# A router that exponentiates all six logits on GpSimd, and output rounding, residual adds and normalization at other steps of the feed-forward loop

## The chip, the cores and the metric

One core of a Trainium2 chip runs the whole program. The metric is the device time of one execution in microseconds (us); lower is better. The engines are named as in the profile: PE (TensorE matmul), PEld (its weight load), DVE (VectorE), ACT (ScalarE), POOL (GpSimd), SP (SyncE, which only issues DMA here).

## What is computed

Two transformer layers over x of 4 x 1024 tokens with 256 features: cross-attention, a mixture of six experts, a second cross-attention, and a quantized feed-forward part, each on a layer-normalized x and each added to x. What matters here are the router and the last part:

```
z = x @ proj_w.T ; q = tanh(z / 0.3) ; dot = q @ anchors.T
logits = -(6 - dot) * 0.5 / clip(routing_temp, 0.1)
topk_logits, topk_idx = top_k(logits, 2)
topk_w = softmax(topk_logits)            # weight 0 for the other four experts
out = sum over e of  gelu(x @ w1[e]) @ w2[e] * weight[e]
...
h = round256(x @ w1 + b1) ; h = round256(piecewise_linear_gelu(h))
out = round256(h @ w2 + b2) ; x = x + out
```

## The kernel before

The 4096 tokens are eight blocks g = 0 to 7 of 512 tokens (NT = 4 tiles of 128 partitions). x stays in SBUF. Four stages follow one another: attention (to about 245 us of the span), experts (250 to 430), attention again (430 to 617), feed-forward (617 to the end). Each engine's program is written out by hand, in order; engines wait for each other on semaphores only, and each engine issues strictly in its written order.

**Experts.** Per block, for e = 0 to 5: PE computes `hidden` (6 matmuls, line 141) and, two experts behind, `output` (12 matmuls, line 640); ACT applies Gelu twice; DVE or POOL forms the low part (`rest` line 598, `rest_pooled` line 509); DVE's `add` (line 608, four instructions a call) adds the expert's output, scaled by the routing weight, into x. PE's `output` of expert e waits until `add` of expert e-1 has emptied the bank. The router of a block is DVE's `router` (in the step e = 0, lines 562 to 578): logits, ten comparisons that give each logit's `rank`, the maximum `top`, `below` = logit - top, and, by way of `second` (rank equal 1, times below) and a sum, `gap`, one number per token: how far the second logit lies below the first. POOL's `power` (line 515) raises e to `gap`, 128x4 elements. DVE's `share` (step e = 2, behind `rest` of that step and ahead of `add` of expert 0, lines 584 to 591) makes the six weights of it: ex at rank 1, 1 at rank 0, over 1 + ex. POOL's other `pow` is line 103, the inverse square root of the normalization, also 128x4, with the product `shift` (line 105) behind it.

**Feed-forward.** The loop runs over k = 0 to 63, with g, c = divmod(k, 8): block g, hidden slice c of 128. "Step c" below is one turn of that loop on one engine. A slice goes: PE `hidden(k)` (6 matmuls, L141), DVE `early(k)` (fixed, L753), ACT two Gelus (fg, L728, L729), POOL `climb(k)` (frise, L711), DVE `interpolate(k)` (fpart, L759), POOL `grow(k)` (fy, L718; on DVE, L765, for c = 1 and 4), ACT `leading(k)` (L735, L738), DVE `rest(k)` (fyl, L771), PE `output(k)` (12 matmuls, L804). In step k the engines do: DVE early(k), interpolate(k-2), rest(k-4), then finish(k-2) where that is DVE's; ACT gelus(k), leading(k-3); POOL climb(k), grow(k-1); PE hidden(k), output(k-6). PE's hidden(k) waits for early(k-2), since two banks are in turn.

Between these stand the pieces of other blocks. DVE's `moments` for block g+2 (stats, L90) is in step 2, POOL's `invert` (L103, L105) in step 4, ACT's `norm` for block g+2 (xn, L114, four tiles) in steps 6 and 7, two tiles each. PE turns the normalized block (`norm.turn`, four transposes, L127) in step 1 of the next block and again in step 5; ACT takes them over with `lead` (L132) first thing in steps 2 and 6, DVE with `norm.rest` (L136) first thing in steps 3 and 7. PE's first hidden of a block needs both. When the outputs of a block are all summed, ACT's `round_output` (fr, L744, two instructions) and then DVE's `ff.add` (x, L780, two instructions) finish it: for block g-2 in step 2 and step 4 of block g. SP stores the block after the add.

Of the kernel before, what the change touches and what calls it, by code (L numbers as in the profile page):

```python
# [16 lines left out]
P = 128  # L17
# [415 lines left out]
class Experts:  # L433
# [5 lines left out]
    def __init__(self, nc, sem, place, norm, ps, m):  # L439
# [23 lines left out]
        self.euler = small("euler", [P, NT, 1], F32)  # L463
# [3 lines left out]
        self.gap, self.ex = small("gap", [P, NT, 1], F32), small("ex", [P, NT, 1], F32)  # L467
        self.exs, self.second = small("exs", [P, NT, E], F32), small("second", [P, NT, E], F32)
# [44 lines left out]
    def power(self, pool, g):  # L513
        pool.wait_ge(self.below_ready, g + 1)
        self.nc.gpsimd.tensor_tensor(self.ex[:], self.euler[:], self.gap[:], ALU.pow).then_inc(self.ex_ready, 1)
        pool.wait_ge(self.ex_ready, g + 1)
# [42 lines left out]
    def router(self, dve, g):  # L559
        nc = self.nc  # L560
        dve.wait_ge(self.dot_done, g + 1)
        nc.vector.tensor_scalar(self.logit[:], self.RD[:, 0:NT * E].rearrange("p (t e) -> p t e", e=E), 6.0, self.half[:, 0:1],
                                ALU.subtract, ALU.mult).then_inc(self.logit_ready, 1)
        dve.wait_ge(self.logit_ready, g + 1)
        for o in range(E):
            for lo, hi, op in ((0, o, ALU.is_gt), (o + 1, E, ALU.is_ge)):
                if lo < hi:
                    self.put(nc.vector.tensor_tensor(self.above[:, :, lo:hi, o], self.logit[:, :, o:o + 1].to_broadcast([P, NT, hi - lo]),
                                                     self.logit[:, :, lo:hi], op))
        self.put(nc.vector.reduce_max(self.top[:], self.logit[:], AX.X))  # L570
        dve.wait_ge(self.router_chain, self.chain)
        self.put(nc.vector.reduce_sum(self.rank[:], self.above[:], AX.X))
        self.put(nc.vector.tensor_tensor(self.below[:], self.logit[:], self.top[:].to_broadcast([P, NT, E]), ALU.subtract))
        dve.wait_ge(self.router_chain, self.chain)
        self.put(nc.vector.scalar_tensor_tensor(self.second[:], self.rank[:], 1.0, self.below[:], ALU.is_equal, ALU.mult))
        dve.wait_ge(self.router_chain, self.chain)
        need(dve, self.ex_ready, g)
        nc.vector.reduce_sum(self.gap[:], self.second[:], AX.X).then_inc(self.below_ready, 1)

    def share(self, dve, g):  # L580
# [3 lines left out]
        self.put(nc.vector.scalar_tensor_tensor(self.second[:], self.rank[:], 1.0, self.ex[:].to_broadcast([P, NT, E]), ALU.is_equal,  # L584
                                                ALU.mult))
        self.put(nc.vector.tensor_scalar(self.total[:], self.ex[:], 1.0, None, ALU.add))
        dve.wait_ge(self.router_chain, self.chain)
        self.put(nc.vector.scalar_tensor_tensor(self.exs[:], self.rank[:], 0.0, self.second[:], ALU.is_equal, ALU.add))
# [245 lines left out]
def build(nc, d, out):  # L834
    m, at0, at1 = memory_map()
    place = Places(nc)
    with ExitStack() as stack:
# [48 lines left out]
        with nc.Block() as block:  # L886
# [219 lines left out]
            def _(act):  # L1106
# [138 lines left out]
                for k in range(BLOCKS * FC):  # L1245
# [9 lines left out]
                    if k < 2:  # L1255
                        norm.norm(act, LN_FFN + 1, range(2 * k, 2 * k + 2))
                    elif c >= FC - 2 and g + 2 < BLOCKS:
                        norm.norm(act, LN_FFN + g + 2, range(2 * (c - FC + 2), 2 * (c - FC + 3)))
                    if c == 2 and g > 1:
                        ff.round_output(act, g - 2)  # L1260
                    if k == BLOCKS * FC - 1:
                        ff.round_output(act, g - 1)
# [5 lines left out]
            def _(dve):  # L1268
# [160 lines left out]
                for k in range(BLOCKS * FC):  # L1429
# [16 lines left out]
                    if c == 4 and g > 1:  # L1446
                        ff.add(dve, g - 2)
# [262 lines left out]
```

## Time and profile before

| | us |
|---|---|
| median of 3 runs (840.4 to 841.5) | 840.44 |
| the profiled execution | 840.4 |
| its span, first to last instruction | 838.6 |
| busy: PE / DVE / ACT / POOL | 756.9 / 673.2 / 521.0 / 352.4 |
| mean granted TensorE clock | 0.979 |

The profile is of one execution. Its span leaves 1.8 us of its time outside the first and last instruction. In a timeline row the columns are start, duration, engine, line, operation, what is written from what, and in brackets how long the engine sat idle before it and what released it. A pipelined matmul's duration overlaps the next one's, so the distance between starts is what counts.

### The profile page before, as it was taken

What the parts mean: (1) busy time and instruction counts of PE and PEld (TensorE: products, weight loads), DVE (VectorE), ACT (ScalarE), POOL (GpSimd) and SP (SyncE); (2) the same over time, 40 slices, a digit from 0 to 9 for tenths busy, and PEclk for the clock granted to TensorE, in tenths of its full rate; (3) what the DMA queues carried; (4) which work ended last, traced back from release to release, by engine and by line L of the source; (5) the groups of instructions that cost most, each with busy time, mean ns of one, the idle gap of its engine ahead of it and who ended that gap; (6) DMA issues with size and microseconds to landing.
All of it is one profiled execution on the core that took longest, in us unless ns stands there. A gap on an engine that the chain in (4) does not pass through costs nothing.

```text
span 838.6 us, 13625 instructions
## 1 busy us (share of the span) xinstructions
PE 756.9 (90%) x4388; PEld 555.8 (66%) x4388; DVE 673.2 (80%) x1614; ACT 521.0 (62%) x943; POOL 352.4 (42%) x309
## 2 busy tenths in 40 slices
PE   3799999999989999999979898888888989988995
PEld 2566566665558888888854555444457978887885
DVE  7657777777877878888886888887869898889896
ACT  4355555555654446554445766666659878988875
POOL 5433322233112222233231222232238988988984
PEclk9899999999999999999987999999999999999999
DMA  7975633564110000001084555754200000000001
GB/s 221 153 181 115 140 65 65 109 113 92 54 33 1 1 1 6 2 1 52 1 125 67 65 76 78 127 73 56 29 1 2 1 26 1 26 27 26 26 11 65
DMA packets 24957, 48.51 MB, mean 58 GB/s; under 512 B 3670, under 2 KB 6871, under 8 KB 24376
## 3 DMA queue, kind: packets, MB, share of 16 engines
q1 hardware_dynamic: 23366, 46.54, 28.9%
q10 hardware_dynamic: 1522, 1.11, 0.4%
q8 instruction: 36, 0.59, 0.3%
q14 instruction: 33, 0.27, 0.1%
HBM read 11.99 MB, written 4.19 MB: 19 GB/s over the span
## 4 chain that ended last, share of the span: by engine, by line
PE 53%; DVE 20%; issue 9%; ACT 7%; DMA 5%; POOL 4%; DVEq 0%; ACTq 0%; POOLq 0%
PE bank L141 15%; PE bank L640 6%; PE bank L377 6%; PE bank L427 6%; PE bank L402 6%; DMA qst<-mt 5%; PE bank L413 4%; DVE mx L333 4%; PE bank L804 3%; PE bank L405 2%; DVE x L608 2%; PE bank L127 2%; DVE fpart L759 2%; POOL fy L718 2%; PE bank L380 2%
## 5 line engine op out<-in xcount | busy, mean ns | idle before, releaser
L307 ACT ACTIVATE pt<-bank 77x512 f32<-77x512 f32 x256 | 146.5, 589 | 119.6 <-PE bank L405 73.2
L333 DVE TENSOR_REDUCE mx<-bank 128x4 f32<-128x308 f32 x256 | 109.2, 471 | 30.6 <-PE bank L380 17.8
L402 PE MATMUL bank<-qst,l_kst 128*77 128x512 f32 (+1 forms) x256 | 107.3, 432 | 19.8 <-DMA qst<-mt 14.0
L377 PE MATMUL bank<-l_kblk,qh 128*128 128x308 f32 x256 | 90.7, 372 | 12.6 <-DVE mx L333 9.0
L711 POOL TENSOR_TENSOR frise<-fg,fg 128x512 f32<-128x512 f32 x64 | 96.1, 1502 | 7.5 <-ACT fg L729 2.7
L402 PEld LDWEIGHTS bank<-qst,l_kst 128*77 128x77 f32 (+1 forms) x256 | 36.9, 149 | 84.0 <-issue 47.6
L377 PEld LDWEIGHTS bank<-l_kblk,qh 128*128 128x128 f32 x256 | 50.7, 199 | 55.9 <-issue 45.7
L103 POOL TENSOR_TENSOR rstd<-var,minus_half 128x4 f32<-128x4 f32 x32 | 34.4, 1075 | 120.5 <-DVE var L98 67.5
L608 DVE SCALAR_TENSOR_TENSOR x<-bank,eweight,x 128x256 f32<-128x256 f32 x192 | 79.5, 476 | 4.6 <-PE bank L640 4.3
L718 POOL TENSOR_TENSOR fy<-fpart,fg 128x512 f32<-128x512 f32 x48 | 72.6, 1513 | 19.4 <-DVE fpart L759 8.7
L283 POOL TENSOR_TENSOR ol<-ot,oh 128x512 fp32r<-128x512 f32 x32 | 41.5, 1296 | 92.6 <-ACT oh L312 60.4
L804 PE MATMUL bank<-fw2h,fyh 128*128 128x256 f32 x256 | 72.5, 283 | 3.4 <-DVE fyl L771 3.3
L413 PE MATMUL bank<-pt,l_vall 128*32 128x512 f32 x512 | 69.3, 613 | 4.7 <-DVE ut L341 2.0
L114 ACT ACTIVATE xn<-x,shift,rstd 128x256 f32<-128x256 f32 (+1 forms) x128 | 66.9, 589 | 10.8 <-POOL shift L105 10.8
L804 PE MATMUL bank<-fw2l,fyh 128*128 128x256 f32 x256 | 72.1, 282 | 0.0
L804 PE MATMUL bank<-fw2h,fyl 128*128 128x256 f32 x256 | 71.9, 281 | 0.0
L759 DVE SCALAR_TENSOR_TENSOR fpart<-ffixed,frise 128x512 f32<-128x512 uint16 x64 | 55.3, 864 | 15.1 <-POOL frise L711 15.0
L141 PE MATMUL bank<-fxh,fw1h 128*128 128x512 f32 x128 | 52.6, 411 | 12.2 <-DVE fxl L136 7.2
L640 PE MATMUL bank<-ew2h,ehh 128*128 128x256 f32 x192 | 56.5, 294 | 2.8 <-DVE x L608 2.8
L728 ACT ACTIVATE fg<-ffixed 128x512 f32<-128x512 int16 x64 | 40.2, 628 | 23.8 <-DVE ffixed L753 23.6
L509 POOL TENSOR_TENSOR ehl<-eh,ehh 128x512 fp32r<-128x512 f32 x16 | 20.7, 1294 | 81.2 <-ACT ehh L525 81.2
L640 PE MATMUL bank<-ew2l,ehh 128*128 128x256 f32 x192 | 54.7, 285 | 0.0
(181 smaller groups left out, 2125.2 us busy)
## 6 DMA issues: line engine op xcount, KB each, us to landing
qst<-qh SPq DMA_DIRECT2D x64, 256.0 KB, 6.8
qst<-ql SPq DMA_DIRECT2D x32, 256.0 KB, 9.0
out<-x SPq DMA_DIRECT2D x8, 512.0 KB, 2.6
qst<-ml SPq DMA_DIRECT2D x8, 480.0 KB
x<-in_x SPq DMA_DIRECT2D x3, 1024.0 KB, 12.5
weights<-in_mlp_w SPq DMA_DIRECT2D x2, 1024.0 KB, 5.0
mraw<-in_mask SPq DMA_DIRECT2D x8, 154.0 KB
x<-in_x SPq DMA_DIRECT2D x2, 512.0 KB, 5.9
```

Of the source, the lines that this page charges most:

```text
L141: last = self.nc.tensor.matmul(out, w, a, start=(first and k == 0), stop=(k == len(ops) - 1))
L307: self.nc.scalar.activation(self.pt[0:T, i // 4 % 2, i % 4, :], self.bank_of(G, i)[0:T, :], ACT.Exp).then_inc(self.probs, 1)
L333: self.nc.vector.reduce_max(out, banks[u % len(banks)][:, 0:4 * T].rearrange("q (p par t) -> q p par t", p=2, par=2), AX.X).then_inc(self. ...
L377: last = self.nc.tensor.matmul(bank, self.qh[:, c, tile], keys, start=True, stop=not layer.masked)
L402: last = self.nc.tensor.matmul(out, layer.kst[rows, layer.stack(c * HC + 2 * k + par), b * T:(b + 1) * T], self.qst[rows, self.slot(G), c ...
L413: last = self.nc.tensor.matmul(self.U[32 * k:32 * k + 32, :], layer.vall[:, self.batch(G), layer.value(c * HC + 2 * k + par), :], self.pt[ ...
L608: last = self.nc.vector.scalar_tensor_tensor(tile, part, self.weight[:, g % 2, 2 * k + t, e:e + 1], tile, ALU.mult, ALU.add)
L640: last = self.nc.tensor.matmul(self.OUT[k][:, t * D:(t + 1) * D], a[:, e % self.R, tile], w[:, e, :], start=(j == 0), stop=(j == 2))
L711: self.nc.gpsimd.tensor_tensor(self.rise[:, k % 2, :], self.g1[:, k % self.R, :], self.g0[:, k % self.R, :], ALU.subtract).then_inc(self.r ...
L718: self.nc.gpsimd.tensor_tensor(self.y[:, k % 2, :], self.part[:, k % 2, :], self.g0[:, k % self.R, :], ALU.add).then_inc(self.y_ready[0], 1)
L759: self.nc.vector.scalar_tensor_tensor(self.part[:, k % 2, :], self.fractions[:, k % self.R, :, 0], 2.0 ** -16, self.rise[:, k % 2, :], ALU ...
L804: last = nc.tensor.matmul(self.OUT[2 * (g % 2) + t // 2][:, t % 2 * D:(t % 2 + 1) * D], a[:, k % self.R, t * P:(t + 1) * P], w[:, c, :], s ...
```

## The change

Router: `gap` and `second` are gone. POOL's pow takes `below` itself, so 128x24 elements (all six logits of each token) and not 128x4, with `euler` as wide. `share` keeps the values where rank is under 2, sums the six, inverts the sum and multiplies.

Feed-forward: ACT normalizes one tile in step 6, one in step 7, and the last two in step 0 of the next block (before: two and two in steps 6 and 7). ACT's `round_output` of block g-1 stands in step 7 of block g, behind that tile (before: step 2 of block g+1). DVE's `ff.add` of block g-2 stands in step 0 of block g (before: step 4).

```diff
-        self.euler = small("euler", [P, NT, 1], F32)
+        self.euler = small("euler", [P, NT, E], F32)
...
-        self.gap, self.ex = small("gap", [P, NT, 1], F32), small("ex", [P, NT, 1], F32)
-        self.exs, self.second = small("exs", [P, NT, E], F32), small("second", [P, NT, E], F32)
+        self.ex, self.exs = small("ex", [P, NT, E], F32), small("exs", [P, NT, E], F32)
...
-        self.nc.gpsimd.tensor_tensor(self.ex[:], self.euler[:], self.gap[:], ALU.pow).then_inc(self.ex_ready, 1)
+        self.nc.gpsimd.tensor_tensor(self.ex[:], self.euler[:], self.below[:], ALU.pow).then_inc(self.ex_ready, 1)
...
         self.put(nc.vector.reduce_sum(self.rank[:], self.above[:], AX.X))
-        self.put(nc.vector.tensor_tensor(self.below[:], self.logit[:], self.top[:].to_broadcast([P, NT, E]), ALU.subtract))
-        dve.wait_ge(self.router_chain, self.chain)
-        self.put(nc.vector.scalar_tensor_tensor(self.second[:], self.rank[:], 1.0, self.below[:], ALU.is_equal, ALU.mult))
-        dve.wait_ge(self.router_chain, self.chain)
         need(dve, self.ex_ready, g)
-        nc.vector.reduce_sum(self.gap[:], self.second[:], AX.X).then_inc(self.below_ready, 1)
+        nc.vector.tensor_tensor(self.below[:], self.logit[:], self.top[:].to_broadcast([P, NT, E]),
+                                ALU.subtract).then_inc(self.below_ready, 1)
...
-        self.put(nc.vector.scalar_tensor_tensor(self.second[:], self.rank[:], 1.0, self.ex[:].to_broadcast([P, NT, E]), ALU.is_equal,
-                                                ALU.mult))
-        self.put(nc.vector.tensor_scalar(self.total[:], self.ex[:], 1.0, None, ALU.add))
+        self.put(nc.vector.scalar_tensor_tensor(self.exs[:], self.rank[:], 2.0, self.ex[:], ALU.is_lt, ALU.mult))
         dve.wait_ge(self.router_chain, self.chain)
-        self.put(nc.vector.scalar_tensor_tensor(self.exs[:], self.rank[:], 0.0, self.second[:], ALU.is_equal, ALU.add))
+        self.put(nc.vector.reduce_sum(self.total[:], self.exs[:], AX.X))
+        dve.wait_ge(self.router_chain, self.chain)
         self.put(nc.vector.reciprocal(self.rtotal[:], self.total[:]))
...
                     if k < 2:
                         norm.norm(act, LN_FFN + 1, range(2 * k, 2 * k + 2))
+                    elif c == 0 and g + 1 < BLOCKS:
+                        norm.norm(act, LN_FFN + g + 1, range(2, NT))
                     elif c >= FC - 2 and g + 2 < BLOCKS:
-                        norm.norm(act, LN_FFN + g + 2, range(2 * (c - FC + 2), 2 * (c - FC + 3)))
-                    if c == 2 and g > 1:
-                        ff.round_output(act, g - 2)
-                    if k == BLOCKS * FC - 1:
+                        norm.norm(act, LN_FFN + g + 2, range(c - FC + 2, c - FC + 3))
+                    if c == FC - 1 and g > 0:
                         ff.round_output(act, g - 1)
...
-                    if c == 4 and g > 1:
+                    if c == 0 and g > 1:
                         ff.add(dve, g - 2)
```

On DVE, the router and the share of block 0 before, from `below` on (line 358 is a residual add of the attention, only in block 0):

```order
L573 TENSOR_TENSOR ebelow<-elogit,etop 128x24
L575 SCALAR_TENSOR_TENSOR esecond<-erank,ebelow 128x24
L578 TENSOR_REDUCE egap<-esecond 128x4
L598 TENSOR_TENSOR ehl<-eh,ehh 128x512
L358 TENSOR_TENSOR x<-x,bank 128x512 x2
L598 TENSOR_TENSOR ehl<-eh,ehh 128x512
L584 SCALAR_TENSOR_TENSOR esecond<-erank,eex 128x24
L586 TENSOR_SCALAR etotal<-eex 128x4
L588 SCALAR_TENSOR_TENSOR eexs<-erank,esecond 128x24
L589 RECIPROCAL ertotal<-etotal 128x4
L591 TENSOR_TENSOR eweight<-eexs,ertotal 128x24
```

and the same place of the change:

```order
L573 TENSOR_TENSOR ebelow<-elogit,etop 128x24
L593 TENSOR_TENSOR ehl<-eh,ehh 128x512
L358 TENSOR_TENSOR x<-x,bank 128x512 x2
L593 TENSOR_TENSOR ehl<-eh,ehh 128x512
L580 SCALAR_TENSOR_TENSOR eexs<-erank,eex 128x24
L582 TENSOR_REDUCE etotal<-eexs 128x4
L584 RECIPROCAL ertotal<-etotal 128x4
L586 TENSOR_TENSOR eweight<-eexs,ertotal 128x24
```

Two instructions ahead of the pow and one in the share are gone; three of the share's four now each need the one before.

On ACT, from the end of step 6 to the end of step 7 before:

```order
L114 ACTIVATE xn<-x,shift,rstd 128x255 x2
L728 ACTIVATE fg_154<-ffixed 128x512
L729 ACTIVATE fg_155<-ffixed,fsegment 128x512
L735 ACTIVATE bank<-fy 128x512
L738 ACTIVATE fyh<-bank 128x512
L114 ACTIVATE xn<-x,shift,rstd 128x255 x2
```

and of the change, from the end of step 6 to the end of step 0:

```order
L114 ACTIVATE xn<-x,shift,rstd 128x255
L723 ACTIVATE fg_152<-ffixed 128x512
L724 ACTIVATE fg_153<-ffixed,fsegment 128x512
L730 ACTIVATE bank<-fy 128x512
L733 ACTIVATE fyh<-bank 128x512
L114 ACTIVATE xn<-x,shift,rstd 128x255
L739 ACTIVATE fr<-bank 128x512 x2
L723 ACTIVATE fg_152<-ffixed 128x512
L724 ACTIVATE fg_153<-ffixed,fsegment 128x512
L730 ACTIVATE bank<-fy 128x512
L733 ACTIVATE fyh<-bank 128x512
L114 ACTIVATE xn<-x,shift,rstd 128x255 x2
```

Two of the four tiles have moved behind leading of step 0, and the two roundings (fr) stand in step 7, where before they stood three steps later.

On DVE, steps 3 (its end) and 4 of a block before:

```order
L765 TENSOR_TENSOR fy<-fpart,fg_154 128x512
L753 TENSOR_SCALAR ffixed<-bank 128x512
L759 SCALAR_TENSOR_TENSOR fpart<-ffixed,frise 128x512
L771 SCALAR_TENSOR_TENSOR fyl<-bank,fyh 128x512
L780 SCALAR_TENSOR_TENSOR x<-fr,x 128x512 x2
```

and steps 0, 1 and the beginning of 2 of the change:

```order
L748 TENSOR_SCALAR ffixed<-bank 128x512
L754 SCALAR_TENSOR_TENSOR fpart<-ffixed,frise 128x512
L766 SCALAR_TENSOR_TENSOR fyl<-bank,fyh 128x512
L775 SCALAR_TENSOR_TENSOR x<-fr,x 128x512 x2
L748 TENSOR_SCALAR ffixed<-bank 128x512
L754 SCALAR_TENSOR_TENSOR fpart<-ffixed,frise 128x512
L766 SCALAR_TENSOR_TENSOR fyl<-bank,fyh 128x512
```

The two adds into x now stand between rest of step 0 and early of step 1.

## Rows read from the trace of the kernel before

**Rows 1.** Busy time by stage: stretch, its length, each engine's busy time, clock, DMA.

```profile
250.00:420.00 170.00, 167.21 (x1053) 142.04 (x1054) 141.51 (x490) 86.59 (x164) 45.90 (x46) 1.00 0.03 9
640.00:800.00 160.00, 148.56 (x947) 133.33 (x947) 141.15 (x239) 136.24 (x244) 140.48 (x98) 1.00 0.05 18
```

**Rows 2.** Waits of PE, 250 to 420 us: total, times, longest.

```profile
PE bank L640 <- DVE x L608: 2.8, 8, 1.2
```

**Rows 3.** Timeline of DVE, share of block 2, router and share of block 3.

```profile
300.58 0.17 DVE L584 SCALAR_TENSOR_TENSOR esecond<-erank,eex 128x24 f32<-128x24 f32 x1
...
317.99 0.17 DVE L573 TENSOR_TENSOR ebelow<-elogit,etop 128x24 f32<-128x24 f32 x1
318.20 0.18 DVE L575 SCALAR_TENSOR_TENSOR esecond<-erank,ebelow 128x24 f32<-128x24 f32 x1
...
318.51 0.68 DVE L598 TENSOR_TENSOR ehl<-eh,ehh 128x512 fp32r<-128x512 f32 x1
...
321.73 0.18 DVE L584 SCALAR_TENSOR_TENSOR esecond<-erank,eex 128x24 f32<-128x24 f32 x1
321.82 0.16 DVE L586 TENSOR_SCALAR etotal<-eex 128x4 f32<-128x4 f32 x1
322.02 0.19 DVE L588 SCALAR_TENSOR_TENSOR eexs<-erank,esecond 128x24 f32<-128x24 f32 x1
...
322.54 1.66 DVE L608 SCALAR_TENSOR_TENSOR x<-bank,eweight,x 128x256 f32<-128x256 f32 x4
```

**Rows 4.** Timeline of POOL, 265 to 320 us.

```profile
269.17 1.01 POOL L103 TENSOR_TENSOR rstd<-var,minus_half 128x4 f32<-128x4 f32 x1 [2.35 <-issue]
270.25 0.32 POOL L105 TENSOR_TENSOR shift<-minus_mean,rstd 128x4 f32<-128x4 f32 x1
...
295.42 1.32 POOL L515 TENSOR_TENSOR eex<-eeuler,egap 128x4 f32<-128x4 f32 x1 [2.60 <-DVE egap L578]
...
318.74 1.32 POOL L515 TENSOR_TENSOR eex<-eeuler,egap 128x4 f32<-128x4 f32 x1 [2.76 <-DVE egap L578]
```

**Rows 5.** Timeline of DVE, feed-forward, blocks 1 to 3, and the tail.

```profile
649.78 1.40 DVE L90 BATCH_NORM_STATS2 stats<-x 128x6 f32<-128x256 f32 x4
...
670.39 0.69 DVE L759 SCALAR_TENSOR_TENSOR fpart<-ffixed,frise 128x512 f32<-128x512 uint16 x1 [1.20 <-POOL frise L711]
...
673.66 0.69 DVE L759 SCALAR_TENSOR_TENSOR fpart<-ffixed,frise 128x512 f32<-128x512 uint16 x1 [1.24 <-POOL frise L711]
...
674.87 1.39 DVE L90 BATCH_NORM_STATS2 stats<-x 128x6 f32<-128x256 f32 x4
...
682.73 3.16 DVE L780 SCALAR_TENSOR_TENSOR x<-fr,x 128x512 f32<-128x512 f32 x2
685.80 0.68 DVE L753 TENSOR_SCALAR ffixed<-bank 128x512 int32<-128x512 f32 x1
...
701.41 1.39 DVE L90 BATCH_NORM_STATS2 stats<-x 128x6 f32<-128x256 f32 x4
...
829.74 1.28 DVE L780 SCALAR_TENSOR_TENSOR x<-fr,x 128x512 f32<-128x512 f32 x2
```

**Rows 6.** Timeline of PE, same stretch: a turn of step 1, and its two stalls.

```profile
669.59 0.60 PE L127 MATMUL bank<-ident,xn 128*128 128x128 f32 x4
...
686.63 0.47 PE L141 MATMUL bank<-fxh,fw1h 128*128 128x512 f32 x1 [1.49 <-DVE ffixed L753]
...
690.99 0.50 PE L141 MATMUL bank<-fxh,fw1h 128*128 128x512 f32 x1 [1.30 <-DVE fxl L136]
```

**Rows 7.** Timeline of ACT: end of step 7, start of steps 0 and 1, block 2.

```profile
667.76 1.08 ACT L114 ACTIVATE xn<-x,shift,rstd 128x255 f32<-128x255 f32 x2
668.75 0.62 ACT L728 ACTIVATE fg<-ffixed 128x512 f32<-128x512 int16 x1
...
670.99 0.62 ACT L728 ACTIVATE fg<-ffixed 128x512 f32<-128x512 int16 x1
```

**Rows 8.** Timeline of POOL: the climbs of steps 2 and 3, block 2.

```profile
678.33 3.32 POOL L711 TENSOR_TENSOR frise<-fg,fg 128x512 f32<-128x512 f32 x2
```

## The prediction

> **What bounds the kernel now.** I read the stretches first. In the expert stage PE is busy 167.2 of 170 us and POOL only 45.9 [rows 1]; PE's only wait there is for DVE's add of expert 0, 2.8 us in eight waits [rows 2]. So anything that delays that add adds to the time one for one, and what shortens DVE's or POOL's own work gives almost nothing. In the feed-forward all four engines are busy 85 to 93% [rows 1], so none bounds it alone and the timelines must be read step by step. Block 1 has no ff.add; from its statistics to those of block 2 are 674.87 - 649.78 = 25.09 us. From there on every block has an add, and 701.41 - 674.87 = 26.54 us pass [rows 5]. The add of step 4, 3.16 us on DVE [rows 5], therefore costs 1.45 us a block. It holds up early of step 5 (685.80), and with it PE's hidden of step 7 (stall 1.49) and, by way of the late norm.rest, the first hidden of the next block (1.30) [rows 6].
>
> **Router, ahead of the pow.** The issue distances are 0.21 us for an instruction that waits for the one before and 0.10 for one that doesn't. Two instructions go: from below to the next ehl are 318.51 - 317.99 = 0.52 us [rows 3], afterwards 0.10. The pow is released 0.42 us sooner in each of 8 blocks. DVE's own 3.4 us are worth nothing, since PE doesn't wait for DVE there.
>
> **Share.** Before: five instructions, 322.54 - 321.73 = 0.81 us, two of them side by side (0.09 and 0.10, the others 0.20 and more) [rows 3]. After: four, each waiting for the one before, 4 x 0.21 = 0.84. Neutral; it stands ahead of the add that PE waits for, so 8 x 0.03 = 0.2 us lost at most.
>
> **The pow, six times as wide.** This is the open price. Trace: 1.32 us for 128x4 in the router, 1.01 for 128x4 in the normalization; the product of 128x4 right behind takes 0.32 [rows 4]. No wider pow is in the trace. Lower end: all of it is fixed, and 20 more columns cost what a subtraction's columns cost on POOL (3.32 us for two of 512 columns [rows 8], 3 ns each): 1.38 us. Upper end: all but the 0.32 of an instruction as such grows with the columns: (1.32 - 0.32) x 6 + 0.32 = 6.3; if the 0.31 by which the router's pow exceeds the other is a wait for a shared access and stays fixed, (1.01 - 0.32) x 6 + 0.63 = 4.8. What covers it: in block 3 the pow starts at 318.74, the share at 321.73: 2.99 us, and 0.42 more from the earlier release, so a pow up to 3.4 us is free. In block 2 it is 300.58 - 295.42 + 0.42 = 5.6 [rows 3, 4]. I count seven blocks like block 3 and one like block 2. The cost is 7 x (d - 3.4): nothing up to 3.4 us, 9.8 us at 4.8, 7 x 2.9 + 0.7 = 21.0 at 6.3. Of these ends neither is nearer to a row: each is the 128x4 row carried on by another assumption. I take the middle between 1.38 and 4.8, 3.1 us, which is just covered, so a cost of nothing; that stands for about 0.4 us of set-up in the pow beside the 0.32, the rest growing with the columns. It is a choice and not a finding, and both ends stay in the range.
>
> The Trainium skill ("GPSIMD Engine Reference", section 2.1) says that a GpSimd tensor_tensor is an ordinary loop over the elements in software. The trace agrees for subtraction (3 ns a column over 512) and has no second width for pow. By that rule pow's extra would lie in the loop: the first rival below, whose price is worked out from the rows above.
>
> **ff.add to step 0.** What it gives where it leaves: at most the 1.45 us a block above, six blocks (2 to 7), 8.7 us. What it costs where it goes: in steps 1 and 2 of a block DVE waits 1.20 and 1.24 us for POOL [rows 5]. The add (3.16) uses these 2.44 and pushes step 2's moments back 0.5 to 0.7. POOL isn't hurt at once: grow of step 0 starts well over 2 us after the interpolation it needs. The adds could run in 1.28 us together, as in the tail where POOL has stopped [rows 5], but steps 7 to 2 are where POOL is never idle, so I keep 3.16. The add also waits for the roundings, now one step ahead of it on ACT and not two: 0.2 us.
>
> **Norm and rounding on ACT.** Steps 6 and 7 lose two tiles (1.0 us), step 7 gets the two roundings (1.0), so Gelu of step 0 starts about where it did, 668.8 to 669.3 [rows 7]. Before, normalization was complete at 668.8 and PE turned at 669.59 without a wait [rows 6]. Now the last two tiles stand behind the plain step of 670.99 - 668.75 = 2.24 us [rows 7] and take 1.0: complete at about 672.6. PE stands still some 3 us in its step 1, a new wait, and behind it is hidden of step 2, done at 674.6. DVE's early of step 2 would have come at 673.5 (its delay by the add counted), so it slips another 1.1; moments then are 1.6 late, early of step 3 too, and POOL, whose climb of step 3 follows that of step 2 directly [rows 8], waits 1.2 for it. Then step 4 has no add: early of step 5 comes at 684.5, not 685.80 (gain 1.3). Working the same steps through the next block with the same durations I get 710.2 against 685.80 + 26.54 = 712.34 (0.8 more). PE profits later, because the stall of 3 us has taken the place of the 1.49 and 1.30: its first hidden of block 3 comes at 690.7 against 690.99, that of block 4 at 717.1 against 717.53 (0.4). For blocks 4, 5 and 6 I take DVE's 0.8 each: 2.9 us when block 7 starts. Block 7 has no norm and no turn, its add is mostly covered before and after: 0.5. Sum 3.4 us. Store DMAs go out four steps sooner, and nothing waits for them but the end, whose last add doesn't move. The tail is the same.
>
> **Sum.** Profiled execution 840.4 (median 840.44, the same), of it span 838.6: minus 3.4 for the feed-forward, plus 0 for the pow, plus 0.2 for the share: **837.2 us**.
>
> **Rivals.** (1) *The pow is a loop.* Against it: only a guess on set-up. For it: nearly 0.7 us more than a product for only four columns. From d = 3.4 on, share waits for POOL, add of expert 0 waits behind it, and PE's output of expert 1 stands. At d = 4.0 the cost is 4.2 and the whole 841.4; at 4.8 it is 9.8 and 847.0; at 6.3 it is 21.0 and 858.2. Slower than before from d = 3.9 on. (2) *The add is wholly absorbed*, the turn's wait falling in PE's slack: 25.09 a block, 8.7 gained, 831.9. For it: in block 1 to 2 PE ran a whole block with no stall. Against: ACT's order puts two tiles on the turn's path in every block. (3) *The turn is the new bound.* PE needs 26.54 - 1.49 - 1.30 = 23.75 a block without stalls; with all 3 us of the turn's wait kept, 26.75, 0.2 more than before: 841.6 in all. It decides if ACT's steps 7 and 0 run no earlier relative to PE than now.
>
> **How the numbers follow.** Forecast with a cheap pow (836 to 839): 0.43. Rival 1: 0.33, of it a third below 841 (the feed-forward's gain pays), a third 841 to 846, a third above. Rival 2: 0.12. Rival 3: 0.12, near 840 to 842. About 0.2%, 1.7 us, is what a measurement can tell from no change. Faster than 838.7: 0.40 of the forecast, 0.12, and 0.03 of rival 1, that is 0.55. Within 0.2% (838.7 to 842.1): 0.03 + 0.10 + 0.08 = 0.21. Slower: 0.20 + 0.04 = 0.24. The range 833 to 847 leaves out a part of rival 2 (0.07) and the upper end of rival 1 (0.10).
>
> **What would show it.** The pow's duration in the changed trace, against 3.4; a wait of share's first instruction for POOL, or PE's wait for L608's successor above 0.35 each. In the feed-forward: a wait of DVE's first moved add for ACT's rounding (0.2 us), PE waiting 2 to 3 us at the transposes of step 1, the two stalls of rows 6 gone, and statistics to statistics 25.7 us. The prediction is wrong if the pow takes over 4 us, or if the turn's wait is either absent or adds to the old stalls.

## The result and the profile after

The changed kernel takes 850.15 us (median of five runs, 847.73 to 856.15) against 841.5 us of the kernel before (five runs, 840.4 to 843.17): a ratio of 1.0101, interval 1.0065 to 1.0137. It is slower by about 8.6 us, outside the predicted range. Its profiled execution took 849.2 us, of it a span of 847.4. The time given with a run is the median of all its executions; its ratio, and every count of clocks below, leaves out those more than 1.5% above the fastest of the same kernel, six in all: two of some 1403 us, and four of kernels with the new feed-forward order, at mean clocks of 0.966 to 0.970, so that the ratios rather flatter that order.

From the first router logits to the last, the expert stage took 401.13 - 249.98 = 151.15 us before and 410.77 - 253.03 = 157.74 now: 6.6 us more. Four of the seven blocks between them take 1.36 to 1.39 us more, two 0.29 and 0.77, one nothing; the share of the last block, behind the last logits, waits too and adds 1.4, which makes 8.0 us. From the first statistics of the feed-forward to the last add: 834.27 - 626.31 = 207.96 us before, 843.06 - 637.26 = 205.80 now, 2.2 us less. The stage ahead of both, whose code is the same, ended 3.05 us later in this trace; the traces of this study with that stage unchanged put the moment anywhere from 249.98 to 253.8, so this is variation between executions and no effect. The three make up the difference of the two profiled executions: 3.05 + 8.0 - 2.2 = 8.85 us, against 849.2 - 840.4 = 8.8.

Against [rows 1], the same two stretches of the changed kernel (stretch, its length, busy time of PE, PEld, DVE, ACT, POOL with the number of instructions, granted clock, DMA):

```profile
250.00:420.00 170.00, 159.68 (x1001) 134.52 (x1000) 131.77 (x441) 84.97 (x161) 70.98 (x44) 1.00 0.02 8
640.00:800.00 160.00, 146.81 (x936) 131.89 (x937) 150.16 (x243) 140.19 (x249) 137.86 (x99) 1.00 0.05 18
```

In the expert stage PE is busy 7.5 us less and POOL 25 us more. Against [rows 2], the waits of PE and then of DVE in the expert stage (total, times, longest):

```profile
PE bank L635 <- DVE x L603: 10.3, 9, 1.5
```

```profile
DVE ehl L593 <- ACT ehh L524: 23.0, 22, 2.7
DVE eexs L580 <- POOL eex L514: 7.0, 7, 1.2
```

PE's wait for the add of expert 0 went from 2.8 us to 10.3, and DVE has a new wait, for the pow, in seven of eight blocks. Against [rows 3, 4], the line of the pow, its duration in ns (shortest, median, longest):

```profile
L514 POOL TENSOR_TENSOR eex<-eeuler,ebelow x8: 4167/4700/4704, 254.9 to 412.6; 128x24 f32<-128x24 f32 x8
```

And one block, POOL, DVE and PE, each row with start and duration, and in brackets the idle time ahead of it and what ended it:

```profile
323.05 4.70 POOL L514 TENSOR_TENSOR eex<-eeuler,ebelow 128x24 f32<-128x24 f32 x1 [2.34 <-DVE ebelow L573]
```

```profile
322.73 0.17 DVE L573 TENSOR_TENSOR ebelow<-elogit,etop 128x24 f32<-128x24 f32 x1
323.04 0.69 DVE L593 TENSOR_TENSOR ehl<-eh,ehh 128x512 fp32r<-128x512 f32 x1
...
327.78 0.18 DVE L580 SCALAR_TENSOR_TENSOR eexs<-erank,eex 128x24 f32<-128x24 f32 x1 [1.24 <-POOL eex L514]
328.00 0.18 DVE L582 TENSOR_REDUCE etotal<-eexs 128x4 f32<-128x24 f32 x1
328.21 0.18 DVE L584 RECIPROCAL ertotal<-etotal 128x4 f32<-128x4 f32 x1
328.43 0.18 DVE L586 TENSOR_TENSOR eweight<-eexs,ertotal 128x24 f32<-128x24 f32 x1
328.64 0.48 DVE L603 SCALAR_TENSOR_TENSOR x<-bank,eweight,x 128x256 f32<-128x256 f32 x1
```

```profile
329.67 0.36 PE L635 MATMUL bank<-ew2h,ehh 128*128 128x256 f32 x1 [1.50 <-DVE x L603]
```

The chain is the one of the first rival: pow, DVE's wait of 1.24 us, four chained share instructions 0.22, 0.21, 0.22 and 0.21 us apart, the add, and 1.50 us of PE standing still.

In the feed-forward, PE's turns against [rows 6] (step 1 of block 1, step 5, and step 1 of block 2), its waits, and DVE and POOL at the places of [rows 5, 8]:

```profile
658.05 0.65 PE L127 MATMUL bank<-ident,xn 128*128 128x128 f32 x4 [1.16 <-ACT xn L114]
669.77 0.60 PE L127 MATMUL bank<-ident,xn 128*128 128x128 f32 x4
683.87 0.66 PE L127 MATMUL bank<-ident,xn 128*128 128x128 f32 x4 [1.79 <-ACT xn L114]
```

```profile
PE bank L127 <- ACT xn L114: 10.3, 6, 1.9
PE bank L799 <- DVE fyl L766: 3.8, 5, 1.3
```

```profile
687.91 1.40 DVE L90 BATCH_NORM_STATS2 stats<-x 128x6 f32<-128x256 f32 x4
...
706.03 2.39 DVE L775 SCALAR_TENSOR_TENSOR x<-fr,x 128x512 f32<-128x512 f32 x2 [0.28 <-ACT fr L739]
...
711.85 0.69 DVE L748 TENSOR_SCALAR ffixed<-bank 128x512 int32<-128x512 f32 x1 [1.14 <-PE bank L141]
...
713.69 1.39 DVE L90 BATCH_NORM_STATS2 stats<-x 128x6 f32<-128x256 f32 x4
```

```profile
718.39 1.57 POOL L706 TENSOR_TENSOR frise<-fg,fg 128x512 f32<-128x512 f32 x1 [1.33 <-ACT fg L724]
```

The two old stalls of 1.49 and 1.30 us [rows 6] are gone, PE waits up to 1.9 us at the turn of step 1 instead, and a block takes 713.69 - 687.91 = 25.78 us where it took 26.54 [rows 5].

### The profile page after: what moved, and what is told of

Its sections match the earlier page's. It is cut to its first block, busy times and chain, and to the rows that moved or that the text cites. A ratio compares the mean times of both kernels' runs of the same rounds, so it can differ in the third digit from the quotient of the medians.

```text
span 847.4 us, 13594 instructions
## 1 busy us (share of the span) xinstructions
PE 758.7 (90%) x4388; PEld 556.8 (66%) x4388; DVE 671.9 (79%) x1590; ACT 521.9 (62%) x943; POOL 377.9 (45%) x309
## 4 chain that ended last, share of the span: by engine, by line
PE 54%; DVE 19%; POOL 8%; issue 7%; ACT 6%; DMA 6%; ACTq 0%; DVEq 0%; POOLq 0%
PE bank L141 15%; PE bank L402 6%; PE bank L377 5%; PE bank L427 5%; PE bank L635 5%; DMA qst<-mt 5%; PE bank L413 4%; DVE mx L333 4%; POOL eex L514 4%; PE bank L799 4%; PE bank L405 2%; DVE fpart L754 2%; PE bank L127 2%; POOL frise L706 2%; DVE x L603 2%
## 5 line engine op out<-in xcount | busy, mean ns | idle before, releaser
L706 POOL TENSOR_TENSOR frise<-fg,fg 128x512 f32<-128x512 f32 x64 | 99.2, 1550 | 13.4 <-ACT fg L724 8.9
L713 POOL TENSOR_TENSOR fy<-fpart,fg 128x512 f32<-128x512 f32 x48 | 67.6, 1408 | 13.5 <-DVE fpart L754 10.2
L754 DVE SCALAR_TENSOR_TENSOR fpart<-ffixed,frise 128x512 f32<-128x512 uint16 x64 | 61.8, 966 | 9.2 <-POOL frise L706 9.2
L635 PE MATMUL bank<-ew2h,ehh 128*128 128x256 f32 x192 | 56.6, 295 | 10.3 <-DVE x L603 10.3
L635 PE MATMUL bank<-ew2h,ehl 128*128 128x256 f32 x192 | 54.5, 284 | 0.0
L522 ACT ACTIVATE eh<-bank 128x512 f32<-128x512 f32 x48 | 28.7, 597 | 39.7 <-PE bank L141 38.6
L799 PEld LDWEIGHTS bank<-fw2h,fyh 128*128 128x128 f32 x256 | 48.3, 189 | 7.2 <-DVE fyl L766 4.8
```

The source lines that it names most:

```text
L635: last = self.nc.tensor.matmul(self.OUT[k][:, t * D:(t + 1) * D], a[:, e % self.R, tile], w[:, e, :], start=(j == 0), stop=(j == 2))
L706: self.nc.gpsimd.tensor_tensor(self.rise[:, k % 2, :], self.g1[:, k % self.R, :], self.g0[:, k % self.R, :], ALU.subtract).then_inc(self.r ...
L713: self.nc.gpsimd.tensor_tensor(self.y[:, k % 2, :], self.part[:, k % 2, :], self.g0[:, k % self.R, :], ALU.add).then_inc(self.y_ready[0], 1)
L754: self.nc.vector.scalar_tensor_tensor(self.part[:, k % 2, :], self.fractions[:, k % self.R, :, 0], 2.0 ** -16, self.rise[:, k % 2, :], ALU ...
L799: last = nc.tensor.matmul(self.OUT[2 * (g % 2) + t // 2][:, t % 2 * D:(t % 2 + 1) * D], a[:, k % self.R, t * P:(t + 1) * P], w[:, c, :], s ...
```

## The experiments

A period below is the distance from one block's statistics to the next one's; "feed-forward" is the distance from its first statistics to the last add; ratios, with their 95% interval, are to the kernel before on the same chip, so that two runs on different chips compare by their ratios and not by their times.

### Which half costs

**The router half alone**: the exponentials of the changed kernel, the feed-forward of the kernel before.

```
-        self.nc.gpsimd.tensor_tensor(self.ex[:], self.euler[:], self.gap[:], ALU.pow)
+        self.nc.gpsimd.tensor_tensor(self.ex[:], self.euler[:], self.below[:], ALU.pow)
```

> The kernel before with the router's half of the change alone: pow on 128x24, share of four instructions, feed-forward untouched. Theory 'pow duration': the pow takes 4.7 us where 3.34 are covered, so about 1.37 us in each of seven blocks less a looser block 2, near +8 us over the kernel before (ratio 1.009 to 1.010); PE's waits for DVE's scaled add in the expert stage sum to about 10 us and not 2.8. Rival 'two halves in conflict': the loss comes from the feed-forward half or from both together, and this kernel is less than 4 us slower.

850.93 us, ratio 1.0101 (1.0081 to 1.0121). First to last logits 157.71 us, feed-forward 207.91 as before; PE's wait for the add 10.3 us. The whole loss of the change is here.

**The feed-forward half alone**, with the router of before.

```
+                    elif c == 0 and g + 1 < BLOCKS:
+                        norm.norm(act, LN_FFN + g + 1, range(2, NT))
...
-                        norm.norm(act, LN_FFN + g + 2, range(2 * (c - FC + 2), 2 * (c - FC + 3)))
-                    if c == 2 and g > 1:
-                        ff.round_output(act, g - 2)
-                    if k == BLOCKS * FC - 1:
+                        norm.norm(act, LN_FFN + g + 2, range(c - FC + 2, c - FC + 3))
+                    if c == FC - 1 and g > 0:
+                        ff.round_output(act, g - 1)
...
-                    if c == 4 and g > 1:
+                    if c == 0 and g > 1:
```

> The kernel before with the feed-forward half alone: tiles 1, 1, 2 in steps 6, 7, 0, rounding in step 7, add in step 0. Theory: the changed kernel's trace has the stretch from the first feed-forward statistics to the last add 2.2 us shorter (205.8 against 208.0), so this kernel is 2 us faster than the one before (ratio 0.997 to 0.998). Rival: the gain of the trace is a product of the later start and the kernel is within 1 us of before; or the half costs and explains part of the loss.

842.2 us, ratio 0.9988 (0.9967 to 1.001): no difference that this can tell. Its profiled execution took 838.49 us, with 151.15 us of experts and a feed-forward of 205.72, so 2.2 us shorter, as expected. The whole series gained less than that one execution and than the 0.997 to 0.998 expected, and the later copies of this kernel, below, show one reason.

**Adds and roundings moved, normalization where it was**, and **the normalization moved alone**.

> The kernel before with rounding in step 7 and the add in step 0, but all four tiles normalized in steps 6 and 7 as before. Theory: the turn of PE's step 1 no longer waits 1.8 us for ACT in each block and block 1 loses nothing, so this is faster than the feed-forward half whole: 3 to 6 us under the kernel before, statistics to statistics near 25.3 us. Rival: two tiles and two roundings in step 7 (about 4.3 us of ACT) are too much for one step; the Gelu of step 0 and the wait of the add for the rounding come a us later, and it is no faster than the feed-forward half whole.

> The kernel before with the tiles moved alone (1, 1, 2 in steps 6, 7, 0), rounding in step 2 and add in step 4 as before. Theory: PE waits 1 to 1.2 us at the turn of step 1 and the add's stalls of steps 7 and 0 stay, but a part of the waits overlap: 1 to 4 us slower than the kernel before. Rival: ACT's freed us in steps 6 and 7 bring norm.rest forward and pay for the turn: within 1 us.

Adds and roundings: 840.79 us, ratio 0.9979 (0.9962 to 0.9996), so barely faster than before and not by the 3 to 6 us expected; feed-forward 207.41, with a period of 26.53 us in the middle blocks, as before. PE now waits 6.5 us in eight times for DVE's early. In these blocks, taking the add out of step 4 gave nothing of the 1.45 us a block: it costs the same again where it goes. Only behind the last statistics is this trace shorter, 76.96 us to the last add instead of 79.79. The normalization alone: 845.65 us, ratio 1.003 (1.0013 to 1.0047), feed-forward 211.18, 3.2 us longer. Its waits of PE after 640 us show why:

```profile
PE bank L127 <- ACT xn L114: 7.8, 6, 1.4
PE bank L141 <- DVE fxl L136: 6.0, 5, 1.3
```

The turn's new wait comes on top of the old one for norm.rest, as the third rival had it. Only with both moves does the turn's wait stand in the place of the old stalls. The two are not additive: +3.2 and -0.5 apart, -2.2 together. The -0.5 is too small a gain, though. In that trace PE's clock fell twice, which the traces of the other two don't have (start and end of the stretch, its length, busy times as above, clock third from the end):

```profile
638.00:640.00 2.00, 2.00 (x9) 1.81 (x8) 2.00 (x4) 1.66 (x4) 1.92 (x2) 0.50 0.00 0
826.00:828.00 2.00, 2.00 (x10) 2.00 (x11) 0.59 (x1) 1.20 (x2) 1.84 (x3) 0.51 0.00 0
```

The first fall alone made the first period 24.89 us where it is 23.47 before, 1.4 us more. By that estimate the adds and roundings gain about 2 us by themselves, nearly what both moves gain together, and that with the second fall not priced. By the ratios, too, the whole half isn't shown to be better than they are alone.

### What a wide pow costs

**The router of before with a wider pow.** gap and its result get three, and then six, columns for each tile. The added columns hold -1.5 and are not used; all other instructions are those of before.

```
-        self.euler = small("euler", [P, NT, 1], F32)
+        self.euler = small("euler", [P, NT, 3], F32)
...
-        self.gap, self.ex = small("gap", [P, NT, 1], F32), small("ex", [P, NT, 1], F32)
+        self.gap, self.ex = small("gap", [P, NT, 3], F32), small("ex", [P, NT, 3], F32)
```

> The arithmetic and instruction order of the kernel before, but the router's pow runs over 128x12 (eight columns of it idle data nobody reads), so only its duration grows; the release isn't 0.42 us earlier. Theory 'pow is a loop' from 4.70 us at 24 columns and 1.32 at 4 (0.169 us a column): 2.7 us, which the 2.99 us up to the share cover: no change in the expert stage (151.15 us from the first logits to the last, as before) and none in PE's wait for DVE's scaled add (2.8 us). Rival 'any longer pow costs at once': stage longer by up to 7 x 1.35 us.

> As the 12-column one with 24 columns: pow 4.7 us. Theory 'only the pow's duration costs': 4.70 - 2.99 = 1.7 us in each of the blocks like block 3, first to last logits 151.15 + 6 x 1.75 less what block 2 has spare (about 160.5 us), and the whole near +11 us; more than the router's half of the change (157.7 us), since the pow is released 0.42 us later. Rival 'the shorter router or the new share costs': this kernel is not slower than 2 us.

With 12 columns: pow 2.58 us, 842.43 us, ratio 0.9992 (0.998 to 1.0004), first to last logits 151.17 us, PE's wait 2.8 as in [rows 2]. With 24: pow 4.48 us, 851.22 us, ratio 1.0096 (1.0083 to 1.011), logits 159.65, 8.5 more, and 1.5 more in the share of the last block behind them. The pow's row and DVE's wait for it in the second kernel:

```profile
L515 POOL TENSOR_TENSOR eex<-eeuler,egap x8: 4476/4476/4700, 255.3 to 414.9; 128x24 f32<-128x24 f32 x8
...
DVE esecond L584: 9.5, 7
```

So the width alone does it, with the old values and the old share, and the cover is real: 2.58 us is free, 4.48 isn't. The price by the cover read from before, 7 x (4.48 - 2.99) = 10.4 us, stands against 8.5 + 1.5 = 10.0 in this trace; the whole series is longer by less, 8.3 us between the medians, and the 11 expected were too many. In the changed kernel, where the pow is released 0.42 us sooner, 7 x (4.70 - 3.4) = 9.1 stands against a loss of 8.0. So the earlier release is worth something once the pow is no longer covered: in most blocks the pow is 0.2 us longer, and it costs 2 us less.

**The pow by itself.** Behind the end of the kernel of before, POOL alone at work runs pow on 1, 4, 12, 24 and 96 columns and a product on 4 and 24, each waiting for the one before, for two pairs of values. These instructions are added work, and the time of the whole says nothing.

```
...
+                    for w in (1, 4, 12, 24, 96):
+                        step(nc.gpsimd.tensor_tensor(result[:, 0:w], base[:, 0:w], power[:, 0:w], ALU.pow))
+                    for w in (4, 24):
+                        step(nc.gpsimd.tensor_tensor(result[:, 0:w], base[:, 0:w], power[:, 0:w], ALU.mult))
```

> The kernel before with idle-time instructions on POOL behind the last add, when every other engine is done: pow over 1, 4, 12, 24 and 96 columns for the base e and exponent -1.5, and for the base 0.37 and exponent -0.5, and products over 4 and 24 columns. Its total time is longer by these and says nothing. Theory 'loop': about 0.38 + 0.158 us a column: 0.5, 1.0, 2.3, 4.2, 15.5 us, the same for both pairs of values; the router's extra 0.3 to 0.5 is DVE at work. Rival 'values': the first pair takes 0.3 us more at 4 columns also with DVE still.

Groups of instructions of POOL by shape (busy time of all, mean ns of one, idle time ahead):

```profile
L1119 POOL TENSOR_TENSOR ut<-ut 128x96 f32<-128x96 f32 x2 | 31.3, 15666 | 0.2
L1119 POOL TENSOR_TENSOR ut<-ut 128x24 f32<-128x24 f32 x2 | 8.3, 4162 | 0.2
L1119 POOL TENSOR_TENSOR ut<-ut 128x12 f32<-128x12 f32 x2 | 4.5, 2268 | 0.2
L1119 POOL TENSOR_TENSOR ut<-ut 128x4 f32<-128x4 f32 x2 | 2.0, 1010 | 0.2
L1119 POOL TENSOR_TENSOR ut<-ut 128x1 f32<-128x1 f32 x2 | 1.1, 556 | 0.2
L1121 POOL TENSOR_TENSOR ut<-ut 128x24 f32<-128x24 f32 x2 | 0.5, 234 | 0.2
L1121 POOL TENSOR_TENSOR ut<-ut 128x4 f32<-128x4 f32 x2 | 0.4, 198 | 0.2
```

From 4 to 24 columns pow grows by (4162 - 1010) / 20 = 158 ns a column, from 24 to 96 by 160, and what doesn't grow is 1010 - 4 x 158 = 378 ns. The values make no difference (the five pows take 23.97 us with one pair and 23.98 with the other). The product grows by 36 / 20 = 2 ns a column. In the kernel 0.3 to 0.5 us comes on top (1.32 against 1.01, 4.48 to 4.70 against 4.16), though not always (4.17 in block 4 of the change); the cause of this was not tried.

### What became of the feed-forward's gain

**The whole change and its feed-forward half again**, on another chip, and the half a third time on a third one.

> The changed kernel once more, beside its own half. Theory 'the halves add up': the router's half costs about 8.0 us (first to last logits 157.7, against 151.15, and 1.4 more behind), the feed-forward half gives 2.2, so about 5.8 us over the kernel before (ratio 1.007). Rival 'they conflict': ratio stays at 1.010 as first measured, and the stretch from the first feed-forward statistics to the last add is longer than the 205.8 of its first trace.

> The feed-forward half alone once more, since its first interval (0.9967 to 1.001) does not tell 2.2 us from nothing. Theory: first statistics to last add 205.7 us again and ratio 0.9973. Rival: the gain does not show in the whole (ratio 0.999 or more), because the stages ahead differ by more from run to run.

> The feed-forward half alone, third set, beside the two above. Theory: between 0.997 and 1.004 with a spread of 7 us and more, its trace with none to two stretches at half clock right behind the turn of step 1, each worth 1.3 to 1.8 us. Rival: no such stretch and yet slower than 1.000.

The whole: 851.21 us, ratio 1.0088 (1.0059 to 1.0117), with 157.74 us from first to last logits again but a feed-forward of 209.05 and not 205.80. The half: 845.3, ratio 1.0039 (1.002 to 1.0058), where 0.9973 was expected, and 844.93, ratio 1.001 (0.9977 to 1.0043). Its feed-forward was 210.59 and 212.33 us in these two traces, not 205.72. The granted clock falls in them right behind the turn's wait. Timeline of PE of the second copy, and two stretches from it (columns as above; the clock stands third from the end):

```profile
677.19 0.66 PE L127 MATMUL bank<-ident,xn 128*128 128x128 f32 x4 [2.08 <-ACT xn L114]
677.61 0.58 PE L141 MATMUL bank<-fxh,fw1h 128*128 128x512 f32 x1
677.99 0.63 PE L141 MATMUL bank<-fxh,fw1l 128*128 128x512 f32 x1
678.41 0.63 PE L141 MATMUL bank<-fxl,fw1h 128*128 128x512 f32 x1
678.84 0.63 PE L141 MATMUL bank<-fxh,fw1h 128*128 128x512 f32 x1
```

```profile
678.00:680.00 2.00, 2.00 (x6) 1.62 (x5) 0.14 (x1) 1.92 (x4) 1.92 (x2) 0.50 0.01 2
...
682.00:684.00 2.00, 2.00 (x13) 1.73 (x13) 1.95 (x8) 1.53 (x3) 1.85 (x2) 1.00 0.00 0
```

Matmuls of 512 columns start 0.43 us apart instead of 0.23: PE is at the lower of its two levels, 1.2 and not 2.4 GHz, until about 681.3. The period in which this falls took 27.42 us where that of the trace without a fall took 25.96. The same happened there behind the turns that start at 636 and 782, in the third copy at 635, 676, 755 and 782, and in the repeat of the whole change at 683 and 710, each time where PE had just waited 1.7 us or more. The turns at 636 and 635 are those of block 0, where PE waits 2.7 us in every kernel, so these two falls are not behind a wait that the change made; the fall at 638 in the adds-and-roundings trace is behind the same turn. The wait doesn't always bring the fall: the first traces of the whole change and of its half have the same waits, and the clock stays at 1.00 until the tail. In the feed-forward of the kernel before, of the router half alone and of both wider pows it stays there too, though PE waits 1.97 us at one other place. This is the row before:

```profile
796.79 0.50 PE L141 MATMUL bank<-fxh,fw1h 128*128 128x512 f32 x1 [1.97 <-DVE fxl L136]
```

A mean granted clock below 0.975 over the span was had by 11 of the 32 executions compared of the three copies, and by 1 of 83 of the kernel before on the same three chips. The average over the executions is 0.980, 0.976 and 0.978 for the three copies and 0.982 for the kernel before on each of these chips.

**The wait filled.** Six matmuls like those of a hidden, on the block's own operands, are put ahead of the turn of step 1 in blocks 1 to 6. Their result is overwritten by the turn, and nothing else is changed in the feed-forward half.

```
+                        else:
+                            norm.project(ff.LN[:, :], ff.w1h, ff.w1l, slice(0, P), ff.xh[g % 2], ff.xl[g % 2])
                         norm.turn(pe, LN_FFN + g + 1, 0, ff.LN)
```

> The feed-forward half with six extra matmuls (1.4 us, their result overwritten by the turn) ahead of PE's wait at the turn of step 1 in blocks 1 to 6. They add no result and stand inside the wait of 1.8 us. Theory 'the idle wait lets the clock fall now and then': no stretch at half clock behind that turn, statistics to statistics 25.9 us in every block, ratio 0.996 to 0.998 with less spread than the half itself. Rival 'chips or the stages ahead make the difference': same time and spread as the feed-forward half beside it; rival 'the matmuls cost': 1 us a block slower.

840.39 us (838.24 to 843.73), ratio 0.9987 (0.9969 to 1.0005). The wait of the turn shrinks to 2.3 us in all, the longest 0.5:

```profile
PE bank L127 <- ACT xn L114: 2.3, 5, 0.5
```

The feed-forward takes 205.84 us, with periods of 25.87 to 25.99, so 1.4 us of useless work a block costs nothing there. None of its 12 executions has a mean clock under 0.975 (average 0.982), where the unfilled copy on the same chip has 5 of 10, and no stretch of its feed-forward is at the lower level until PE has finished. Its interval overlaps that of the unfilled copy, so the gain in time isn't shown by the ratios; that the wait brings the clock down in part of the executions is, by the clocks.

### A version that beats both

**The turn in step 2.** The feed-forward half, with PE's turn moved from step 1 to 2, norm.lead to step 3 and norm.rest to step 4.

```
-                    if c == (3 if g == 0 else 1) and g + 1 < BLOCKS:
+                    if c == (3 if g == 0 else 2) and g + 1 < BLOCKS:
...
-                    if c in (4 if g == 0 else 2, 6) and g + 1 < BLOCKS:
+                    if c in (4 if g == 0 else 3, 6) and g + 1 < BLOCKS:
...
-                    if c in (5 if g == 0 else 3, 7) and g + 1 < BLOCKS:
+                    if c in (5 if g == 0 else 4, 7) and g + 1 < BLOCKS:
```

> The feed-forward half of the change (router as before) with PE's first turn of the next block one step later, in step 2, and ACT's lead and DVE's norm.rest after it in steps 3 and 4. Theory 'the turn's wait is what holds the new order back': PE's 1.8 us waits for ACT at the turn go, DVE's waits for PE's hidden with them, statistics to statistics go from 25.9 to about 25.1 us, and first statistics to last add from 205.7 to about 201: 4 to 7 us faster than the kernel before. Rival 'POOL bounds the block': at 25.9 us it is busy 24, and the waits only change places: within 1 us of the feed-forward half alone.

> The late turn with the feed-forward half once more. Theory: its longest wait of PE at a turn is 0.6 us, so no clock falls there, and 4 us (ratio 0.995) under before as in its first set. Rival: the first set was a lucky chip, and it lies within 1 us of before.

838.69 us, ratio 0.9946 (0.9929 to 0.9962), and on another chip 839.53, ratio 0.9962 (0.9941 to 0.9983). Feed-forward 204.27 and 204.15 us, 3.7 less than before, where the expectation had 201; none of 18 executions with a mean clock under 0.975. Its waits of PE and of DVE after 640 us:

```profile
PE bank L804 <- DVE fyl L771: 4.7, 5, 1.7
PE bank L127 <- ACT xn L114: 2.5, 5, 0.6
PE bank L141 <- DVE fxl L136: 2.4, 5, 1.0
```

```profile
DVE fpart L759 <- POOL frise L711: 15.9, 15, 1.7
```

PE's waits of 10.3 us at the turn are down to 2.5, and DVE waits 15.9 us for POOL's climb, 6.3 in the changed kernel. The period falls to 25.7 and not to the 25.1 expected. POOL is now busy 97.1 of the 105 us from 670 to 775 (PE 101.5, DVE 95.8, ACT 91.9); that POOL alone holds the period isn't shown.

**The late turn without the rest of the change.**

> The kernel before with the turn one step later alone (norm, rounding and add where they were). Theory 'the late turn helps only because the new order made PE wait there': the kernel before has no wait at the turn of step 1, so nothing is gained, within 1.5 us of before (statistics to statistics 26.5 us). Rival 'a later turn is better in itself': as much as in the new order, 1.5 us or more faster.

843.43 us, ratio 1.0004 (0.9983 to 1.0025), feed-forward 208.41. Alone it gives nothing: before, PE didn't wait at the turn.

**One more grow on DVE**, that of c = 5, on top of the late turn, to relieve POOL.

```
-    ON_DVE = (1, 4)
+    ON_DVE = (1, 4, 5)
```

> The late turn with the feed-forward half, and one more of the eight additions of a block (c = 5) on DVE and not on POOL. In the late-turn kernel POOL is busy 97.1 of 105 us from 670 to 775. Theory 'POOL bounds it now': statistics to statistics go from 25.73 to about 24.8 us, 5 us faster than the late turn alone, some 9 under the kernel before. Rival 'DVE has no room': it is busy 95.8 of 105; the addition falls into step 7 beside norm.rest, and the time stays or grows.

844.48 us, ratio 1.0024 (1.0006 to 1.0042), feed-forward 211.23, period 27.4. The theory of a gain of 5 us failed and the rival was right: DVE has no room for it. Over the same 105 us POOL's busy time falls to 78.5, DVE's rises to 99.2, and POOL's grow waits 28.1 us for DVE's interpolate instead of 3.9. Relieving the one engine only filled another.

## Why the prediction was wrong, point by point

The prediction was 837.2 us, the measurement 850.15. Two terms of its sum failed: the pow, put at nothing, cost 8.0 us, and the 3.4 us of the feed-forward don't show in the whole. The pow alone wouldn't have carried the time out of the range, since the 9.1 us that the prediction's own formula gives for 4.70 make 846.3. Add the 3.4, take off the 1.1 by which the formula was too high, add the 1.1 by which the kernel before was slower this time (841.5 against 840.44), and it is 849.7; the last 0.5 us stay unexplained.

**The pow's width: the step that failed.** The prediction took 3.1 us, the middle between 1.38 and 4.8, and so a cost of nothing. It is 4.70 us and costs about 8 us. What the step had wrong is the choice, not the bounds: 4.8 was worked out from the pow of the normalization carried on in proportion, with the router's excess of 0.31 us kept fixed, and 4.70 was measured. The choice stood for 0.4 us of set-up beside the 0.32; the measured share that doesn't grow is 0.38 in all, not 0.72, with POOL alone at work. The first rival, with a chance of 0.33, is what happened. Rows 4 could have said more than the text took from them: a pow was 0.69 us longer than a product on the same four columns right behind it, and something that the product doesn't have must either be set-up or work on each column. The Trainium skill ("GPSIMD Engine Reference", section 2.1) speaks of a loop over the elements; probe and padded kernels agree, with 158 ns a column. The prediction weighed it as a rival only.

**The cover.** Right in kind: a pow of 2.58 us is free, 4.48 is not. The price of a block was right, 1.3 us by the formula and 1.36 to 1.39 in four of them; the count of seven such blocks was not. In blocks 0 and 4 DVE waits 0.15 and 0.70 us, and the whole costs 8.0 us instead of 9.1. In block 0 the share comes later (256.11 - 252.25 = 3.86 us behind the start of the pow before, where block 3 has 2.99), and the pow takes 4.48 us; in block 4 the pow takes 4.17. The row of one block had been taken for all.

**Release and share.** Right: in block 3 the pow starts 0.32 us behind below instead of 0.75, so 0.43 us sooner where 0.42 was foreseen. DVE's next split stands 0.31 us behind below, where 0.52 was measured before and 0.10 foreseen. The share takes four steps of 0.21 or 0.22.

**The feed-forward: right mechanism, two terms missing.** The turn's wait was there (1.8 us from block 2 on, not 3), DVE's and POOL's waits too (1.14 and 1.33), the stalls of 1.49 and 1.30 were gone, and the period fell to 25.8 to 26.0 against the 25.7 foreseen. The first missing term is the turn of block 1, of which nothing was said: it waits 1.16 us, and the first period gets 1.2 longer (24.69 against 23.47) with no add to lose in exchange. The second period, into which the first add now falls, gets 0.9 longer (25.96 against 25.09); the prediction had this in its working, as moments 1.6 us late. So an undisturbed trace gains 2.2 us, and by this count would have gained the predicted 3.4 without block 1's turn. That it fits so well is in part luck: the wait of the turn, this delay and the add in its new place (2.39 to 2.86 us, not 3.16) all came out smaller than assumed, and the four terms behind the 2.9 us (0.4 and three times 0.8) only add up to 2.8. The second missing term is the clock: PE's wait brings it down in part of the executions, 1.3 to 1.8 us each time. In the whole nothing of the gain is left to see: ratios of 0.9988, 1.0039 and 1.001. How much of that is the clock's doing the times don't show, since the filled copy, with no fall, comes to 0.9987 with an interval up to 1.0005. The trace of before has waits of 2.71 and 1.97 us in its feed-forward and no fall behind either, so it couldn't show this; that five new waits might cost more than themselves wasn't asked.

**The other rivals.** The add was not absorbed (period 26.53 with adds and roundings moved alone), and the turn as a new bound is what the normalization alone shows, 3.2 us slower, but not the two together.

## What to carry to other kernels

A price that the trace shows at one width only, and that is several times that of another operation of the same shape, grows with the width until shown otherwise: take the proportional end, above all where the cover ends between the two. Widening an operation to save short ones on an engine that nobody waits for had nothing to win here, and stood to lose as soon as the cover was used up. A new wait of PE in a dense stretch is to be looked at for what it does to the granted clock, and moving the waiting step later, beyond what it waits for, repaired it here.

## What the chip showed that was not expected

With POOL alone at work, its pow takes 0.38 us and 0.158 us for each column of 128 partitions, where each column of a product takes 2 ns. PE's clock fell to the lower level in these feed-forward traces behind single waits of 1.7 to 2.7 us (in the trace shown until about 681.3), with PE busy up to them and after, and in the same kernel it didn't behind others of the same length; what decides between the two stays open.
